# A filling stage rebuilt: the first image's norms, convolution and softmax spread over other engines, weights loaded in two transfers, new instruction orders

## The reference, cut to what matters

```
x_ln = layernorm(x) * g + b;  q = x_ln @ wq + bq
o    = gelu(depthwise_conv_7x7_stride_2(q as image) + dw_b)      # 49 taps, 8 x 8 outputs
offs = o @ pw_w;  positions = ref + tanh(offs);  s = bilinear samples of x there   # 64 samples
att  = softmax(q mq (s wv mk)^T) (s wv mv), 8 heads;  z = att @ mo + mo_b + x
t0   = gelu(layernorm(z) @ mlp + mlp_b) + z
t1   = t0 + landmark_attention(ln(t0))          # top 4 of 16 segments per head, softmax
t2   = t1 + expert_layer(ln(t1))                # query norms, top 16 of 64 keys twice,
                                                # top 16 of 256 sums, softmax, 16 experts per head
```

## Time and profile before

| | us |
|---|---|
| three runs | 451.69, 451.50, 449.02 |
| median | 451.5 |
| the profiled execution, its own time | 449.87 |
| its span, first to last instruction | 447.8 |
| busy in the span: DVE | 358.4 (80%) |
| PE matmul, weight loads | 308.1 (69%), 225.2 (50%) |
| POOL | 217.9 (49%) |
| ACT | 140.7 (31%) |
| mean granted TensorE clock, share of full speed | 0.701 |

### The profile page before, as it was taken

One profiled execution on the slowest core, in us unless ns is written; L12 is line 12 of the kernel. 1 busy time (PEld: TensorE's weight loads), 2 busy tenths in 40 slices (PEclk: granted clock), 3 DMA queues, 4 the chain that ended last, 5 costly groups with the idle time before them and its releaser, 6 DMA issues.

```text
span 447.8 us, 7841 instructions
## 1 busy us (share of the span) xinstructions
PE 308.1 (69%) x2275; PEld 225.2 (50%) x2275; DVE 358.4 (80%) x2163; ACT 140.7 (31%) x324; POOL 217.9 (49%) x411
## 2 busy tenths in 40 slices
...
DMA packets 1634, 3.50 MB, mean 8 GB/s; under 512 B 180, under 2 KB 1205, under 8 KB 1592
## 3 DMA queue, kind: packets, MB, share of 16 engines
...
## 4 chain that ended last, share of the span: by engine, by line
DVE 55%; PE 23%; POOL 9%; issue 6%; ACT 6%; DMA 1%; DVEq 0%; ACTq 0%; POOLq 0%
PE bank L876 6%; DVE Sx L1363 5%; DVE i L1369 5%; DVE i L1370 5%; DVE cands L1419 4%; DVE onehot L494 4%; DVE vraw L1366 3%; DVE vraw L1360 3%; DVE segmax L1244 3%; DVE c L1416 3%; PE bank L540 2%; PE bank L550 2%; DVE masked L1426 2%; PE bank L783 2%; ACT hat L914 2%
## 5 line engine op out<-in xcount | busy, mean ns | idle before, releaser
L876 PEld LDWEIGHTS bank<-weights,onehot 108*128 108x128 f16 x1024 | 69.0, 178 | 3.1 <-DVE onehot L494 1.5
L876 PE MATMUL bank<-weights,onehot 108*128 108x16 f16 x1024 | 69.0, 216 | 1.9 <-DVE onehot L494 1.4
L1644 POOL TENSOR_TENSOR inv<-nrm,mhalf 128x16 f32<-128x16 f32 x8 | 23.4, 2925 | 35.8 <-DVE nrm L1376 35.8
L458 POOL TENSOR_TENSOR taps<-qpad,wa 128x128 f32<-128x128 f32 x96 | 36.0, 427 | 2.0 <-ACT qpad L929 1.9
L540 PE MATMUL bank<-wa,hat 128*128 128x128 f32 x24 | 6.7, 371 | 32.9 <-ACT hat L914 32.9
L1557 POOL TENSOR_TENSOR rstd<-veps,mhalf 128x2 f32<-128x2 f32 x16 | 11.7, 731 | 34.6 <-DVE veps L1166 34.3
L1370 DVE FIND_INDEX8 i<-vraw,Sx 128x8 uint16<-128x64 f32 x128 | 28.0, 219 | 0.0
L1369 DVE FIND_INDEX8 i<-vraw,S 128x8 uint16<-128x64 f32 x128 | 28.0, 218 | 0.0
L1363 DVE MATCH_REPLACE8 Sx<-vraw,S 128x64 f32<-128x64 f32 x128 | 25.1, 209 | 0.0
L803 PE MATMUL bank<-KB,qsT 128*128 128x256 f32 x64 | 24.9, 558 | 0.2 <-issue 0.2
L494 DVE TENSOR_SCALAR onehot<-eT 108x512 f16<-108x512 uint16 x84 | 24.4, 366 | 0.0
...
## 6 DMA issues: line engine op xcount, KB each, us to landing
...
bq_row<-rows_dram SPq DMA_DIRECT2D x1, 0.5 KB
...
```

The lines of the kernel that those rows point to most:

```text
L458: ins = eng.tensor_tensor(tv[:, :, :, ky, kx:kx + n], q, dw[:, ky, kx:kx + n].unsqueeze(1).unsqueeze(1).broadcast_to([P, G8, G8, n]), ALU. ...
L876: last = mm(o[:, g * 16:g * 16 + 16], OHv[:, c * NT + t, g], Rv[:, c, t, g, s], start=(c == 0 and s == 0), stop=(c == NCH - 1 and s == 1))
L1644: g_.tensor_tensor(inv[:, n], nrm[:, n], mhalf[:, 0:2 * H], ALU.pow).then_inc(inv_ready, 1)
```

## The change

- `wa` is reordered and loaded in two transfers: first the 441 columns that norm 0, the first projection and the convolution need, then, behind the bias row, the rest. Waits are split in the same way (`wa0_loaded`, `wa_loaded`).
- Three memsets (`qpad`, `rts`, `bias`) go from POOL to DVE.
- Image 0 only: DVE writes the normalized tiles itself (`H0` to `H3`). In norm 0 it multiplies by the gain while POOL computes the power, and the bias `lnb` is added by two more products on PE that run before the tile is there.
- Image 0's convolution: taps 0 to 20 on DVE in four running sums, taps 21 to 34 on ACT, the last 14 on POOL, which also adds its second seven to its first. DVE then adds blocks of taps four times and reduces the four that are left. ACT's copy `qT` comes after its taps.
- Image 0's first softmax: DVE subtracts the maximum into `e0`, ACT takes one exponential of 512 elements for each half in place of eight of 64.
- `NS` is cut in pieces (`NSa` to `NSe` on DVE, `NSa`, `NSb` on POOL), which stay together and at their place. `TG.0`, `TE.0` and `TE.1` are one-element activations that bring a function table in early.
- New orders for PE and ACT in all images; DVE's and POOL's orders differ only by the new and renamed steps. 14 fillers are left of 21. PE's and ACT's order of image 0, and PE's end, are in the diff below; further on, ACT takes `F12.1` ahead of `F5b.2`, `N4.0` after `A0b.3` just ahead of `N0h.1`, and `N4.3` ahead of `N2p.3`; PE takes `F12.0` ahead of `F5c.1`. `BANKS` is new as well.

```diff
-CONV_DVE = 4
+CONV_DVE = 21
+CONV_POOL = 5
+SUMS = 4
...
-    "tensor": """A1a.0 A2d.0 A1b.0 W.0 W.1 A3a.0 A3b.0 A3c.0 A4.0 W.2 W.3 F5a.0 A1a.1 F5c.0 NS.0 F6a.0 F6b.0 W.4 W.5
-        F6c.0 F7a.0 F7b.0 F8a.0 A1b.1 F8b.0 F9b.0 A2d.1 F9a.0 F9c.0 A3a.1 A3b.1 W.6 A3c.1 A4.1 W.7 W.8 F8c.0
...
-        N5a.2 N0f.3 N0e.3 W.15 N5b.2 N0g.3 W.16 N6a.2 W.17 N4.3 N6b.2 N3a.3 N3h.3 N5a.3 W.18 N5b.3 W.19 W.20
-        N6a.3 N6b.3""".split(),
...
+    "tensor": """A1a.0 A2d.0 A1b.0 W.0 W.1 W.2 A3a.0 A3b.0 A3c.0 A4.0 W.3 F5a.0 A1a.1 F5c.0 F6a.0 NS.0 F6b.0 F6c.0 F7a.0
+        F7b.0 A1b.1 W.4 W.5 F8a.0 F8b.0 F9b.0 F9a.0 A2d.1 F9c.0 A3a.1 A3b.1 A3c.1 A4.1 W.6 F8c.0 F9d.0 F10a.0
...
+        N5b.2 N0g.3 N4.3 N6a.2 N6b.2 N3a.3 N3h.3 N5a.3 N5b.3 W.13 N6a.3 N6b.3""".split(),
...
-    "scalar": """A0b.0 A1a.0 A2c.0 A2d.0 A3a.0 A3b.0 A1b.0 A3c.0 A4.0 A0b.1 F5b.0 A1a.1 F5c.0 F6b.0 F7a.0 F7b.0 F8a.0
...
+    "scalar": """A1a.0 A2a.0 A2c.0 A2d.0 A3a.0 A3b.0 A3c.0 A1b.0 A4.0 A0b.1 F5b.0 A1a.1 F5c.0 TG.0 F6b.0 F7a.0 F7b.0
+        F8a.0 F8b.0 A2c.1 A2d.1 F9a.0 A3a.1 A1b.1 A3b.1 A3c.1 TE.0 F8c.0 A4.1 F10a.0 F10b.0 F11t.0 A0b.2 F11b.0
...
-    "vector": """A0a.0 A2c.0 A3a.0 NB.0 A0a.1 F5a.0 NS.0 F6a.0 F6c.0 F7b.0 A2c.1 F8b.0 F9b.0 F9a.0 F9c.0 F9d.0 A0a.2
...
+    "vector": """A0a.0 H0.0 A2c.0 A3a.0 NB.0 A0a.1 F5a.0 NSa.0 NSb.0 NSc.0 NSd.0 NSe.0 F6a.0 F6c.0 H1.0 F7b.0 H2.0 A2c.1
...
-WEIGHTS_A = [("ident", 128), ("wq", 128), ("lng", 128), ("lnb", 128), ("vecs", 8), ("pw", 2), ("less", 2), ("refs", 2),
-             ("iota", 16), ("hm", 8), ("dw", 49), ("wv2", 256), ("mq", 128), ("mk", 128), ("mv", 128),
+WEIGHTS_A = [("wq", 128), ("lng", 128), ("lnb", 128), ("vecs", 8), ("dw", 49), ("ident", 128), ("pw", 2), ("less", 2),
+             ("refs", 2), ("iota", 16), ("hm", 8), ("wv2", 256), ("mq", 128), ("mk", 128), ("mv", 128),
...
+        def add_taps(unit, to, src, n):
+
+            return unit.tensor_tensor(taps[:, to:to + n, :], taps[:, to:to + n, :], taps[:, src:src + n, :], ALU.add)
+
+        def window(k):
+
+            ky, kx = divmod(k, KS)
+            return qpad[:, ky:ky + 15:2, kx:kx + 15:2]
+
+        def tap(k):
+            return taps[:, k, :].rearrange("p (y x) -> p y x", y=G8)
...
+            first = offA["ident"][0]
+            sp.dma_start(wa[:, 0:first], wa_in[:, 0:first]).then_inc(wa0_loaded, 16)
             sp.dma_start(bq_row[0:1, :], rows_in[0:1, 0:C]).then_inc(bq_loaded, 16)
+            sp.dma_start(wa[:, first:NA], wa_in[:, first:NA]).then_inc(wa_loaded, 16)
...
-                    pe.wait_ge(wa_loaded, 16)
+                    pe.wait_ge(wa0_loaded, 16)
...
                 o = take("qimg", b)
                 mm(o[:, 0:N], ones[0:1, :], bq_row[0:1, :].unsqueeze(1).broadcast_to([1, NT, C]), start=True, stop=False)
+                if b == 0:
+                    mm(o[:, 0:N], A("lnb"), A("wq").unsqueeze(1).broadcast_to([P, NT, C]), start=False, stop=False)
+                    oT = take("qT", b)
+                    mm(oT[:, 0:N], A("wq"), A("lnb").unsqueeze(1).broadcast_to([P, NT, C]), start=True, stop=False)
                 pe.wait_ge(xln_ready, b + 1)
                 for s in range(NT):
                     c = slice(s * P, s * P + P)
...
-                o = take("qT", b)
-                last = mm(o[:, 0:N], A("wq"), xln[:, :, :], start=True, stop=True)
+                o = oT if b == 0 else take("qT", b)
+                last = mm(o[:, 0:N], A("wq"), xln[:, :, :], start=(b >= 1), stop=True)
                 done(last, "qT", b)
...
+                    if b == 0:
+                        pe.wait_ge(e0_ready, t + 1)
...
             def normalized(k, src, b):

+                if b == 0:
+                    return
...
+            def TG(b):
+                ac.wait_ge(preset, 1)
+                fn(spare[0:1, 2 * b + 1:2 * b + 2], ones[0:1, 0:1], ACT.Gelu)
...
-                    ac.wait_ge(wa_loaded, 16)
+                    ac.wait_ge(wa0_loaded, 16)
                     ac.wait_ge(preset, 1)
+                    ac.wait_ge(preset_dve, 1)
...
-                o = full(ac, "qT", b)
-                freed(fn(qT[:, :].rearrange("p (c s) -> p s c", s=2),
-                         o[:, 0:N].rearrange("p (s c) -> p s c", s=2), ACT.Identity, bias=vec("bq")), "qT", b)
+                if b >= 1:
+                    copy_qT(b)
+
+            def A2a(b):
+
+                dw = A("dw")
+                read_out(ac, "qimg", b)
+                for k in range(CONV_DVE, CONV_POOL * KS):
+                    last = fn(tap(k), window(k), ACT.Identity, scale=dw[:, k:k + 1])
+                last.then_inc(taps_act_ready, 1)
+                copy_qT(b)
...
-                    ac.wait_ge(negm_ready, NT * b + t + 1)
+                    if b == 0:
+                        read_out(ac, f"S0_{t}", b)
+                        fn(e0[:, t, :], e0[:, t, :], ACT.Exp).then_inc(e0_ready, 1)
+                        continue
+                    ac.wait_ge(negm_ready, NT * (b - 1) + t + 1)
...
-            def statistics(k, src):
+            v.memset(qpad[:, :, :], 0.0)
+            v.memset(rts[:, :, :], LARGE)
+            v.memset(bias[:, :, :, :], 0.0).then_inc(preset_dve, 1)
+            dve.wait_ge(preset_dve, 1)
...
+            def statistics(k, src, b):
...
-                v.tensor_scalar(negmean[:, k, :], mv[:, k, :, 0], -1.0, None, ALU.mult)
+                if b >= 1:
+                    v.tensor_scalar(negmean[:, k, :], mv[:, k, :, 0], -1.0, None, ALU.mult)
...
+            def hats(k, src, b):
+                dve.wait_ge(rstd_ready[k], b + 1)
+                for t in range(NT):
+                    last = v.tensor_scalar(hat[:, k, t, :], src[:, t, :], mv[:, k, t, 0:1], rstd[:, k, t:t + 1],
+                                           ALU.subtract, ALU.mult)
+                last.then_inc(hat_ready[k], 1)
+
+            def H0(b):
+                dve.wait_ge(wa0_loaded, 16)
+                for t in range(NT):
+                    last = v.scalar_tensor_tensor(hat[:, 0, t, :], x_sb[:, b, t, :], mv[:, 0, t, 0:1], A("lng"),
+                                                  ALU.subtract, ALU.mult)
+                link(last)
+                dve.wait_ge(rstd_ready[0], b + 1)
+                for t in range(NT):
+                    last = v.tensor_scalar(xln[:, t, :], hat[:, 0, t, :], rstd[:, 0, t:t + 1], None, ALU.mult)
+                last.then_inc(xln_ready, 1)
+
+            def H1(b):
+                hats(1, z[:, :, :], b)
...
-                    link(conv_rows(v, 0, CONV_DVE))
+                    dw = A("dw")
+                    for k in range(CONV_DVE):
+                        i = k % SUMS
+                        if k < SUMS:
+                            ins = v.tensor_scalar(tap(i), window(k), dw[:, k:k + 1], None, ALU.mult)
+                        else:
+                            dve.wait_ge(sums_ready, k - SUMS + 1)
+                            ins = v.scalar_tensor_tensor(tap(i), window(k), dw[:, k:k + 1], tap(i), ALU.mult, ALU.add)
+                        ins.then_inc(sums_ready, 1)
+                    dve.wait_ge(sums_ready, CONV_DVE)
+                    dve.wait_ge(taps_act_ready, 1)
                 dve.wait_ge(taps_pool_ready, b + 1)
-                n = KS * KS if b == 0 else FOLDED
-                v.tensor_reduce(conv[:, :], taps[:, 0:n, :].rearrange("p k n -> p n k"), X,
+                if b == 0:
+                    link(add_taps(v, 22, 32, 10))
+                    link(add_taps(v, 22, 27, 5))
+                    link(add_taps(v, 21, 24, 3))
+                    link(add_taps(v, 0, 21, 3))
+                v.tensor_reduce(conv[:, :], taps[:, 0:FOLDED, :].rearrange("p k n -> p n k"), X,
                                 ALU.add).then_inc(conv_ready, 1)

...
-                                    negate=True).then_inc(negm_ready, 1)
+                    ov = o[:, :].rearrange("p (h k) -> p h k", h=H)
+                    least = v.tensor_reduce(negM[:, t, :], ov, X, ALU.max, negate=True)
+                    if b >= 1:
+                        least.then_inc(negm_ready, 1)
+                        continue
+                    link(least)
+                    freed(v.tensor_tensor(e0[:, t, :].rearrange("p (h k) -> p h k", h=H), ov,
+                                          negM[:, t, :].unsqueeze(2).broadcast_to([P, H, NP_]), ALU.add), f"S0_{t}", b)

...
-            def NS(b):
+            def NSa(b):
...
-                dve.wait_ge(wb_loaded, 16)
...
+            def NSb(b):
+                k, keys = slice(0, NK), Sw("keys")
...
+            def NSc(b):
+                dve.wait_ge(wb_loaded, 16)
+                dve.wait_ge(rows_loaded, 16)
...
+            def NSd(b):
                 split_rows(offR["fbq"][0], NR)
+
+            def NSe(b):
...
-            g_.memset(qpad[:, :, :], 0.0)
-            g_.memset(rts[:, :, :], LARGE)
-            g_.memset(bias[:, :, :, :], 0.0)
...
+                root = g_.tensor_tensor(rstd[:, k, :], veps[:, k, :], mhalf[:, 0:NT], ALU.pow)
```

(30 more changed lines are left out.)

95 lines of the change are left out of this document (60 added, 35 removed).

## The result

The changed kernel took **455.1 us** by the median of 4 runs (452.77 to 457.13), the kernel before 451.2 on the same chip (449.02 to 451.69). The ratio is 1.0089, with an interval of 1.0056 to 1.0122: about 4 us slower, where 443.0 was forecast. The profiled execution took 452.77, with a span of 451.0; it is the fastest of the four, so its trace shows 2.9 of the 4 us.

The account below looks back on a forecast made before the run. DVE's own work bounds the middle, and image 0's stage chain the start. Gains 1.5 + 3.7 - 0.45 + 0.85 + 0 + 1.55 = 7.15 us off 449.87 give 442.7, stated as 443.0; range 437.5 to 448.5.

Parts of the forecast that it names:

- -0.45: Fillers before image 0's keys and scores: `W.2` costs 0.95 us, one filler fewer before F5a.0 returns 0.5; net loss.
- DVE then writes `hat` in 0.45: Image 0's norm 1: DVE's write takes 0.45 us where shift and ACT took 1.19; norm 1 ends 0.3 early.
- POOL is last: Image 0's convolution: POOL's part takes 4.25 us, DVE's taps 4.0, ACT's 3.0, so POOL finishes last.
- 0.19 an instruction: Image 0's convolution: each of DVE's 21 tap instructions of 64 elements costs 0.19 us, 4.0 us in all.
- Prepares the keys in one piece: After image 0's softmax: two DVE additions, then the keys' preparation in one piece; F6a.0 comes 1.1 us later.
- The start: Image 0's products on the normalized tile begin at 6.8 instead of 8.32, a gain of 1.5 us.
- unchanged within -3 to +4: Middle, first search to last scatter: DVE's and POOL's orders stay the same, gain 0, ends -3 and +4 us.
- the 1.55: Kernel's end: with fewer fillers around the last scatter, PE's last products start 1.55 us earlier.
- the 13 that I had named as a sign of being wrong: Middle: DVE's waits, 12.7 us before, exceeding 13 us would show the steps to be wrong.
- Slow running sums: Rival, image 0's convolution: DVE at 0.34 an instruction, or POOL slowed by it; 2.8 us lost, 445.8; chance 0.13.
- ACT starves DVE in the middle: Rival: ACT's N4 ahead of N0h.1 makes DVE wait; 455 with 12 us added, 448 with 5; chance 0.10.
- around 180: Middle: DVE waiting over 0.3 us for queries around 180 us would show the steps to be wrong.

Follow-up runs that it names:

- experiment 3: Changed kernel plus two POOL waits, so its folds of 1536 and 768 elements for image 1 start only after image 0's hats 1 and 2: 451.1 us, 1.0003.
- experiment 14: Changed kernel with POOL's convolution products of image 0 started only when DVE's 21 taps are done: 454.4 us, one run.
- Experiment 6: Kernel before the change with three filler steps (six passes) taken out between A3b.1 and F10a.0: 453.9 us, 1.0070 of before.
- experiments 2: Changed kernel with image 0's norms 1 to 3 back on ACT with POOL's shift: 453.7 us, 1.0071 of the kernel before.

## Why the prediction was wrong

I forecast image 0 to gain 5.6 us ahead of the first search, and it lost 3.4. The 9.0 between, by stage, from the starts in both traces (gains are positive; F5a.0 and F6a.0 by DVE's start):

| Stage | forecast | measured | missed |
|---|---|---|---|
| to `qpad` | +1.5 | +0.36 | 1.1 |
| `qpad` to conv | +3.7 | +1.6 | 2.1 |
| conv to F5a.0 | -0.45 | -0.7 | 0.2 |
| F5a.0 to F6a.0 | -1.1 | -2.75 | 1.65 |
| F6a.0 to the search | +1.95 | -1.9 | 3.85 |

- **The hats, "DVE then writes `hat` in 0.45": the step that failed most.** They took 3.69 and 2.89, 5.7 us more than forecast, and the rest of the stage gave 1.9 of it back; experiment 3 takes the hold away and returns 4.0 us of time. I costed DVE's instruction as if alone, and POOL's fold of 1536 starts on the same event, the end of `rstd`.
- **The convolution, "POOL is last".** My 0.19 an instruction was right (experiment 14: 0.194). What I left out is that POOL's own part holds DVE's. I had named that contention, charged it to POOL at 0.3 us, and given DVE none; it was 2.4 us on DVE. The additions behind it took 0.82, 0.49, 0.36 and 0.36 us, as added up.
- **The keys' preparation.** "Prepares the keys in one piece" went in at the old length; held by POOL's products it grew to 12.0 us from 10.3, and 9.1 is what it takes alone. The kernel before paid for this too: its three casts took 0.52, 0.59 and 0.77 us.
- **The start.** Tile, transfer and products came as forecast. The table load at 8.01 was missing from the sum: in the kernel before, the first activation's load ran in idle time at 0.72, and the sum has no term for it once that activation has work to wait for.
- **Fillers, middle and end.** -0.45 was -0.7 by DVE's start, -0.5 by that of PE's scores. First search to last index search went from 287.0 to 288.1 us (forecast: unchanged within -3 to +4), the rest from 55.4 to 54.1, a gain of 1.3 for the 1.55. Those terms held, the middle partly by luck. DVE's listed waits in it went from 12.7 to 17.1 us, past the 13 that I had named as a sign of being wrong; DVE's busy time went from 268.4 to 264.8, which the 84 instructions that write `onehot` account for (24.1 us before, 20.2 after, as 18 and 8 of them took over 0.55 us). I had forecast neither. And I costed a removed filler by its own time only. Experiment 6 shows 3.5 us for six passes; by which products is not shown.
- **The rivals.** "Slow running sums" had the right place and a wrong cause. "ACT starves DVE in the middle" did not decide: the waits for queries cost 3.7 us, 1.7 more, not 12, and none of them stood around 180. That its 455 is the measured median is luck.

The rule was there to be read. The Trainium skill, SBUF — State Buffer, section Who interferes with whom, says that VectorE and GpSimd share one pair of ports as an exclusive lock: they contend when VectorE's instruction is in a 2-port mode, or has two SBUF inputs while GpSimd reads SBUF, and whoever issues first has the pair for the whole instruction. The traces agree for the hats and the taps, with an end 0.05 to 0.09 us behind POOL's. In the keys it was worse than that: the cast that started at 39.95, behind a POOL product that ended at 40.19, ended only at 42.00, and four more products of POOL had run and ended by then. I cited its milder form, contention, and priced it from a row in which each instruction of POOL lasts 0.4 us. One in a fold lasts 3.4.

So the hold itself is shown, for the hats, the taps and the keys. Its share of the time is shown less well. In experiments 2 and 3 the hats end alike (52.4 and 52.7; 59.0 both) and the searches come alike (108.06 and 108.13), yet the medians are 453.7 and 451.1. How much the clock takes back in a given order stays open, since no run here holds the clock fixed. And with the hold at the hats, the table load and part of the taps mended, the kernel stands at 447 to 448, not at 443.
